# Two gate stages of a graph network kernel: six product slots, third additions on GpSimd, a place of its own for each fold and sum

## The reference, cut to what matters

```
h3 = h.reshape(B, N, F)                         # B = 8, N = 32, F = 768
hg = einsum('bnf,gf->bng', h3, Wg[:, :F])
qg = einsum('blf,gf->blg', q, Wg[:, F:]) + bg   # 64 tokens
attn = sigmoid(hg[:, :, None, :] + qg[:, None, :, :])
qi = einsum('bnlf,blf->bnf', attn, q)
alpha = sigmoid(h3 @ Wq[:, :F].T + qi @ Wq[:, F:].T + bq)
hn = alpha * tanh(qi) + (1.0 - alpha) * h3
```

## Time and profile before

| | us |
|---|---|
| median of three runs | 818.7 |
| lowest and highest | 816.2, 818.98 |
| span of the profiled execution | 814.7 |
| stage 1, first product to last step's sum | 144.15 |
| stage 2, the same | 145.31 |

### The profile page before, as it was taken

One profiled execution on the slowest core, in us unless ns is written; L12 is line 12 of the kernel. 1 busy time (PEld: TensorE's weight loads), 2 busy tenths in 40 slices (PEclk: granted clock), 3 DMA queues, 4 the chain that ended last, 5 costly groups with the idle time before them and its releaser, 6 DMA issues.

```text
span 814.7 us, 10588 instructions
## 1 busy us (share of the span) xinstructions
PE 771.4 (95%) x4195; PEld 640.1 (79%) x4198; DVE 605.2 (74%) x664; ACT 424.9 (52%) x508; POOL 517.8 (64%) x221
## 2 busy tenths in 40 slices
PE   7999999999988999998898889999999999998998
PEld 4669986776645699776666558999999999976897
DVE  8966249999999640889999997764696488666454
ACT  6424446777674342677676725434443444253742
POOL 0625619999998284699999955770685178805500
PEclk9999999999999999999999999999999999999999
DMA  9037526445332464270153328556356546350001
GB/s 365 33 82 234 164 71 176 91 141 156 116 117 78 122 232 150 58 201 1 63 195 117 116 79 281 185 194 230 108 166 207 181 131 218 117 233 0 2 1 39
DMA packets 24409, 111.01 MB, mean 136 GB/s; under 512 B 3620, under 2 KB 6180, under 8 KB 23976
## 3 DMA queue, kind: packets, MB, share of 16 engines
q1 hardware_dynamic: 23240, 104.24, 39.7%
q10 hardware_dynamic: 1120, 6.10, 2.0%
HBM read 100.63 MB, written 0.79 MB: 124 GB/s over the span
## 4 chain that ended last, share of the span: by engine, by line
PE 62%; DVE 19%; POOL 13%; ACT 3%; issue 2%; DMA 0%; DVEq 0%; ACTq 0%
PE ps L1098 28%; DVE prod L1995 11%; POOL prod L593 8%; PE ps L1064 8%; PE ps L1129 5%; DVE qi_t L2013 4%; PE ps L1611 3%; POOL prod L596 2%; PE ps L1389 2%; PE ps L1256 2%; PE ps L1277 2%; PE ps L1679 1%; PE ps L1436 1%; PE ps L1257 1%; PE ps L1326 1%
## 5 line engine op out<-in xcount | busy, mean ns | idle before, releaser
L581 POOL TENSOR_TENSOR w_lo<-w_raw,w_hi 128x1536 fp32r<-128x1536 f32 x49 | 183.7, 3762 | 141.1 <-ACT w_hi L677 141.0
L593 POOL TENSOR_TENSOR prod<-prod 128x1024 f32<-128x1024 f32 x94 | 223.1, 2396 | 26.8 <-DVE prod L1995 26.6
L810 ACT ACTIVATE prod<-ps 128x1024 f32<-128x1024 f32 x192 | 187.4, 1023 | 68.6 <-PE ps L1389 56.0
L1995 DVE TENSOR_TENSOR prod<-prod,ps 128x2048 f32<-128x2048 f32 x96 | 217.7, 2279 | 5.5 <-ACT prod L810 3.5
L677 ACT ACTIVATE w_hi<-w_raw 128x1536 fp32r<-128x1536 f32 x60 | 88.9, 1488 | 119.1 <-PE ps L1098 108.7
L1389 PE MATMUL ps<-sel_pair,h_and_q 128*128 128x512 f32 x384 | 128.2, 446 | 16.7 <-ACT prod L810 16.5
L1098 PE MATMUL ps<-w_hi,yt_hi 128*128 128x384 f32 x480 | 122.9, 336 | 0.1
L1098 PE MATMUL ps<-w_lo,yt_hi 128*128 128x384 f32 x480 | 121.9, 334 | 0.0
L1098 PE MATMUL ps<-w_hi,yt_lo 128*128 128x384 f32 x480 | 121.8, 334 | 0.0
L1389 PEld LDWEIGHTS ps<-sel_pair,h_and_q 128*128 128x128 f32 x384 | 66.5, 189 | 52.5 <-ACT prod L810 32.3
L1064 PE MATMUL ps<-w_raw,h_t 128*128 128x384 f32 x312 | 106.5, 486 | 0.0
(11 more groups left out here) (260 smaller groups left out, 1104.4 us busy)
## 6 DMA issues: line engine op xcount, KB each, us to landing
w_raw<-weights SPq DMA_DIRECT2D x105, 768.0 KB, 4.4
wa_in<-weights SPq DMA_DIRECT2D x6, 768.0 KB, 5.9
w_gat<-weights SPq DMA_DIRECT2D x6, 768.0 KB, 7.9
w_query<-weights SPq DMA_DIRECT2D x3, 768.0 KB, 11.6
h_and_q<-stage_hi SPq DMA_DIRECT2D x24, 96.0 KB, 2.1
h_and_q<-stage_lo SPq DMA_DIRECT2D x24, 96.0 KB, 2.2
a_vec<-gat_vectors ACTq DMA_DIRECT2D x1, 2048.0 KB, 9.6
q_t<-queries ACTq DMA_DIRECT2D x1, 1536.0 KB, 10.5
```

The costliest lines, as they stand in the source:

```text
L581: pool.tensor_tensor(Wl[:, j, :], raw_slab(U, 0, j), Wh[:, j, :], ALU.subtract).then_inc(w_lo_by_pool, 1)
L593: pool.tensor_tensor(v[:, :, 0:32], v[:, :, 0:32], v[:, :, 32:64], ALU.add).then_inc(folded_once, 1)
L810: act.activation(slot_view(s)[:, :, 32 * u:32 * u + 32], args.rearrange("p b (n l) -> p (b n) l", l=LH), ACT.Sigmoid).then_inc(sigmoid_rea ...
L1995: TT(slot_view(s), slot_view(s), ps[:, 6, o:o + L].unsqueeze(1).broadcast_to([P, NB, L]), ALU.mult).then_inc(products_ready, 1)
```

## The change

1. `PSLOTS` goes from 4 to 6. The first five slots lie over the split weights and on into the next region, the sixth over part of the split state. To make room, `h_t` moves by 6144 bytes, the two halves of `yt_hi` and `yt_lo` change places (`v % 2` becomes `1 - v % 2`), and the attention layers at the end use a view of their own, `h_t_attention`, at the old place.
2. A slot is laid out as two contiguous halves of tokens, [2, 32 nodes, 32 tokens], instead of [32 nodes, 64 tokens]. The sigmoid writes a half in one run, the first addition reads two runs of 1024, and the product reads the query row as two halves.
3. A fourth kind, "H": GpSimd adds 8 to 8 after the second addition (256 numbers), and VectorE sums 8 tokens a node. The kinds are written out step by step (T tensor, V vector, G the old "pool").
4. The fold of each tensor step, the second addition and the sum each have a place of their own, in tables. Every second addition in them stands at its own step. The counting of semaphores follows the tables.
5. There is a path for first additions by DMA (`BY_DMA`); both of its lists are empty, so all first additions are on GpSimd.

```diff
-PSLOTS = 4
+PSLOTS = 6
-FOLD_AT = [(5, 8, 11, 14, 15, 17, 20, 22, 23, 26, 35, 44, 46),
-           (5, 8, 9, 11, 12, 14, 15, 17, 18, 20, 21, 23, 26, 35, 38, 41)]
-ALONE = [(4, 10, 16, 25, 27, 28, 30, 34, 37, 40, 42, 45), (25, 27, 28, 30, 34, 40, 42, 44)]
...
-REST_AT = [[s + (3 if KIND[i][s] == "tensor" and KIND[i][s + 1] != "tensor" else 2) for s in range(STEPS - 1)] for i in range(2)]
+KIND = ["VGGVVTHTGVGTGVTVTHVTHVTGGVHTVVTGTGVVHVTHVTTVGTH",
+        "VGVHVTHTTVTHVTGTTVTGVVVTHGHTVTGTVTGTVGTVGVTGGTH"]
+BY_DMA = [(),
+          ()]
+FOLD_AT = [{8: 5, 11: 7, 14: 11, 17: 14, 20: 16, 23: 19, 26: 22, 31: 27, 34: 30, 35: 32, 41: 38, 44: 41, 46: 42, 47: 45},
+           {8: 5, 10: 7, 12: 8, 14: 10, 17: 13, 19: 15, 21: 16, 23: 18, 26: 23, 31: 27, 34: 29, 35: 31, 38: 33, 40: 35, 41:
+           38, 46: 42, 47: 45}]
...
+REST_AT = [[(), (), (0,), (1,), (2,), (), (4,), (3,), (5,), (6,), (8,), (7, 9), (10,), (), (), (11, 12), (), (13,), (14,),
+           (15, 17), (16,), (18,), (), (19, 20, 21), (), (23,), (22,), (24,), (25, 26), (), (), (27, 28), (), (), (29, 30),
+           (31,), (32, 33, 34), (), (35,), (36, 37), (), (38, 39), (40,), (), (41,), (43,), (42,), (44,), (45, 46)],
+           [(), (), (0,), (), (1, 2), (), (3,), (4,), (5, 6), (), (7,), (9,), (8,), (11,), (10,), (12,), (), (13, 14), (),
+           (15,), (), (16, 17), (19,), (18, 20), (), (21, 22), (24,), (23, 25), (), (), (26,), (27, 28), (), (30,), (29, 32),
+           (31,), (), (), (33, 34), (37,), (35, 36), (38, 39), (), (40,), (), (41,), (42, 43), (44,), (45, 46)]]
...
-        PR = sb("prod", [P, PSLOTS, 2048], F32, wh_off)
+        PR = [sb(f"prod{k}", [P, 2, NB, LH], F32, wh_off + 8192 * k if k < 5 else g_off + 16384) for k in range(PSLOTS)]
-        HT = sb("h_t", [P, KC, N], F32, y_off)
+        HT = sb("h_t", [P, KC, N], F32, y_off + 6144)
+        HA = sb("h_t_attention", [P, KC, N], F32, y_off)
...
+            def first_fold(i, s):
...
+                    pool.tensor_tensor(v[:, 0], v[:, 0], v[:, 1], ALU.add).then_inc(folded_once, 1)
+            def second_fold(i, s):
+                v = slot_view(s)[:, 0]
+                wait_folded(pool, i, s)
+                pool.tensor_tensor(v[:, :, 0:16], v[:, :, 0:16], v[:, :, 16:32], ALU.add).then_inc(folded_twice, 1)
+                if KIND[i][s] == "H":
+                    pool.wait_ge(folded_twice, second(i, s))
+                    pool.tensor_tensor(v[:, :, 0:8], v[:, :, 0:8], v[:, :, 8:16], ALU.add).then_inc(folded_thrice, 1)
...
                     if s >= PSLOTS:
                         if u == 1:
-                            act.wait_ge(folded_once, (STEPS - 1) * i + (s - PSLOTS + 1))
-                        elif KIND[i][s - PSLOTS] == "tensor":
-                            act.wait_ge(fold_ready, count_kind(i, s - PSLOTS, "tensor"))
+                            wait_folded(act, i, s - PSLOTS)
+                        elif KIND[i][s - PSLOTS] == "T":
+                            act.wait_ge(fold_ready, by_tensor(i, s - PSLOTS))
                         else:
-                            act.wait_ge(qi_ready, STEPS * i + (s - PSLOTS + 1))
+                            act.wait_ge(qi_ready, reduced(i, [s - PSLOTS]))
...
-                    for past in (s - 3, s - 2):
-                        if past >= 0 and REST_AT[i][past] == s:
-                            reduce(past)
+                    for past in REST_AT[i][s]:
+                        reduce(past)
...
                 reduce(STEPS - 1)
-                reduce(STEPS - 2)
+                for past in REST_AT[i][STEPS]:
+                    reduce(past)
```

More of the change, by code:

```diff
@@ new lines, with numbered @@
+REST_AT = [[(), (), (0,), (1,), (2,), (), (4,), (3,), (5,), (6,), (8,), (7, 9), (10,), (), (), (11, 12), (), (13,), (14,),
[5 rows of a table added]
+def numbered(keys):
+    return {s: n + 1 for n, s in enumerate(keys)}
+FIRST_BY_POOL = [numbered(s for s in range(STEPS - 1) if s not in BY_DMA[i]) for i in range(2)]
+DMA_BEFORE = [sum(s % PSLOTS == k for s in BY_DMA[0]) for k in range(PSLOTS)]
+SECOND = [numbered(s for at in SECOND_AT[i] for s in at) for i in range(2)]
+THIRD = [numbered(s for s in SECOND[i] if KIND[i][s] == "H") for i in range(2)]
@@ L81 @@
+FOLDED = [numbered(FOLD_AT[i].values()) for i in range(2)]
+REDUCED = [numbered([s for at in REST_AT[i][:STEPS] for s in at] + [STEPS - 1] + list(REST_AT[i][STEPS])) for i in range(2)]
 QUERY_EVENTS = [0, 1, 5, 6]
 HEAD_EVENTS = [(2, 3, 4), (7, 8, 9)]
-BANK7 = [sorted([(s, "fold", s - 3) for s in FOLD_AT[0]] + [(29, "q", 0), (32, "q", 1), (38, "h", 0), (40, "h", 1)]),
-         sorted([(s, "fold", s - 3) for s in FOLD_AT[1]] + [(29, "q", 0), (32, "q", 1), (43, "h", 0), (45, "h", 1)])]
+BANK7 = [sorted([(at, "fold", s) for at, s in FOLD_AT[0].items()] + [(29, "q", 0), (32, "q", 1), (38, "h", 0), (40, "h", 1)]),
+         sorted([(at, "fold", s) for at, s in FOLD_AT[1].items()] + [(29, "q", 0), (32, "q", 1), (43, "h", 0), (45, "h", 1)])]
@@ L321, in build @@
         products_ready = sem("products_ready")
+        dma_folded = [sem(f"dma_folded{k}") for k in range(PSLOTS)]
         folded_once = sem("folded_once")
         folded_twice = sem("folded_twice")
+        folded_thrice = sem("folded_thrice")
         fold_ready = sem("fold_ready")
@@ L422, in place_of, with wait_folded, second, third @@
             return t, f, 4 * t + bb, bb
-        def count_kind(i, s, kind):
-            return sum(k == kind for g in range(i) for k in KIND[g]) + sum(k == kind for k in KIND[i][:s + 1])
+        def wait_folded(eng, i, s):
+            if s in BY_DMA[i]:
+                k = s % PSLOTS
+                before = DMA_BEFORE[k] if i == 1 else 0
+                eng.wait_ge(dma_folded[k], 16 * (before + sum(q % PSLOTS == k and q <= s for q in BY_DMA[i])))
+            else:
+                eng.wait_ge(folded_once, (len(FIRST_BY_POOL[0]) if i == 1 else 0) + FIRST_BY_POOL[i][s])
+        def second(i, s):
+            return (len(SECOND[0]) if i == 1 else 0) + SECOND[i][s]
+        def third(i, s):
+            return (len(THIRD[0]) if i == 1 else 0) + THIRD[i][s]
+        def by_tensor(i, s):
+            return (len(FOLDED[0]) if i == 1 else 0) + FOLDED[i][s]
+        def reduced(i, steps):
+            return STEPS * i + max(REDUCED[i][s] for s in steps)
         def head_views(g):
@@ L644, in _ @@
                 for s in range(STEPS - 1):
-                    fold(i, s)
+                    first_fold(i, s)
+                    for q in SECOND_AT[i][s]:
+                        second_fold(i, q)
                     if s == 34:
@@ L1441, in turn_queries @@
                     bank7_free(at_)
-                    pe.wait_ge(qi_ready, STEPS * i + HALF)
+                    pe.wait_ge(qi_ready, reduced(i, range(HALF)))
                     f0, f1 = ((0, 4), (4, KC))[part]
@@ L2362, in elu @@
                     dve.wait_ge(elu_exp_ready, n)
-                    dve.scalar_tensor_tensor(out=HT[:, ks, half], in0=elu_t[:, ks, half], scalar=-1.0,
+                    dve.scalar_tensor_tensor(out=HA[:, ks, half], in0=elu_t[:, ks, half], scalar=-1.0,
                                              in1=chunk_tile(6 - 2 * t, KC)[:, ks, :], op0=ALU.add,
```

91 lines of the change are left out of this document (48 added, 43 removed).

## The result

The changed kernel takes 815.91 us (median of 18 runs, 815.06 to 817.16) against 818.45 us for the kernel before (18 runs, 815.91 to 819.46): ratio 0.9978, 95% interval 0.997 to 0.9986. The 2.5 us are clear of noise, but they are no change by the 0.5% that the prediction set itself; the time is 2.0 us under the 817.9 forecast and inside its own range of 815.5 to 820.5. The profiled span went from 814.7 to 814.2 us; forecast was 813.9.

The account below looks back on a forecast made before the run. In the two gate stages three engines are nearly full, VectorE and GpSimd fullest. Gains of at most 1.3 and 1.5 us, with 1.0 us idle kept in each, become -0.3 and -0.5, together -0.8: span 813.9, time 817.9, range 815.5 to 820.5.

Parts of the forecast that it names:

- The fold in step 47: End of both gate stages on TensorE: a fold of 1.71 us between query part and turns delays the last turn.
- Idle time of VectorE: Both gate stages: of VectorE's 4.0 and 6.4 us of idle time, 1.0 us stays in each.
- Costs of single operations: Gate stages: third addition 0.75 us, 256-element sum 0.41, first additions 2.4 and products 2.28 as before.
- GpSimd's end: GpSimd's last addition in each gate stage: its end moves from 262.9 and 480.1 to 260.9 and 474.7 us.
- The distance from the span to the median: Whole kernel: the median lies 4.0 us above the profiled span, taken as fixed; span 813.9 gives time 817.9.
- (a): Stage ends: the fold in step 47 costs nothing, engine sums reach the end; -3.0 and -3.2 us, time 812.5; chance 0.20.
- (c): Contiguous halves aren't free: 96 products 0.05 us dearer or cheaper, +4.8 or -4.8, time 822.7 or 813.1; chance 0.08.
- (b): GpSimd's third additions come late and VectorE stands still, 0.6 us for each of 13: +5.0, time 823.7; chance 0.14.

Follow-up runs that it names:

- Run 1: Changed kernel with step 45 of kind V instead of T in both stages, so no fold in step 47: 812.87 us, ratio 0.9945 to the kernel before.
- run 4: Changed kernel with all 13 steps of kind H made G, so no third additions: 818.11 us, ratio 1.0001 to the kernel before.
- runs 2 and 3: Changed kernel with the tables of the kernel before: with six slots 817.96 us, ratio 0.9999; with four slots (layout alone) 818.03 us, 1.0008.

## Why the prediction came out as it did

**The fold in step 47: right.** From product 46's end to the last turn the prediction had 9.57 and 10.2 us; the trace has 9.64 and 10.23, against 7.86 and 6.85 before. Run 1 takes the fold out and gets 1.71 and 1.81 us. In stage 1 that is all that was added. In stage 2 another 1.6 us are: TensorE's last query part waits for the sum of step 43, which VectorE made ahead of product 46 before and makes behind it now. TensorE there, in the kernel before and in the changed one:

```profile
472.36 1.53 PE L1064 MATMUL ps<-w_raw,qi_t 128*128 128x384 f32 x4 [1.02 <-DVE qi_t L2013]
```

```profile
471.79 1.53 PE L1118 MATMUL ps<-w_raw,qi_t 128*128 128x384 f32 x4 [1.79 <-DVE qi_t L2072]
```

The first starts 1.96 us before product 46 ends, the second 1.02 us after it. No experiment moved that sum back. Fold and sum are why a change that puts VectorE 1.5 and 4.8 us ahead gives so little.

**Idle time of VectorE: right in kind, twice the size.** I kept 1.0 us in each stage; it is 2.2 and 2.1 (of the latter 0.8 ahead of the statistics of the gate's first node tile). The choice of 1.0 had no row behind it, and the 6.4 us of stage 2 before were short too: the trace has 6.8, with 0.3 us of sums waiting for GpSimd that the earlier trace rows leave out. Of stage 1's, 1.9 us is waiting for ScalarE's sigmoid; of the 1.4 us in the earlier trace rows none went, though the slot waits of ScalarE itself did (5.6 us before, none after). Six slots alone took these slot waits away too, and left VectorE's idle time as it was but for the fall of the clock: it was not the slots that made ScalarE late.

**Costs of single operations: right.** Third addition 0.73 us (0.75), 256-element sum 0.41 (0.41), first additions 2.39 and products 2.28 as before. GpSimd's end is 1.4 and 4.5 us earlier, where 2.0 and 5.4 were forecast.

**What was left out: VectorE instructions with two SBUF operands beside GpSimd.** By the prediction's terms and the 1.0 us kept, product 46 was to end at 139.15 and 138.2; it ended at 139.63 and 137.18. Stage 1 is half a microsecond worse than the sum, stage 2 a microsecond better. The kernel before, on VectorE and then GpSimd:

```profile
220.86 1.92 DVE L2025 TENSOR_TENSOR tanh_q<-tanh_q,alpha 128x768 f32<-128x768 f32 x1
...
455.97 1.00 DVE L1848 SCALAR_TENSOR_TENSOR small<-small 128x1 f32<-128x1 f32 x1
```

```profile
220.70 1.27 POOL L596 TENSOR_TENSOR prod<-prod 128x512 f32<-128x512 f32 x1
221.93 3.09 POOL L593 TENSOR_TENSOR prod<-prod 128x1024 f32<-128x1024 f32 x1
...
454.58 2.37 POOL L593 TENSOR_TENSOR prod<-prod 128x1024 f32<-128x1024 f32 x1
```

and the changed kernel on VectorE:

```profile
219.93 1.33 DVE L2084 TENSOR_TENSOR tanh_q<-tanh_q,alpha 128x768 f32<-128x768 f32 x1
...
433.53 1.68 DVE L2084 TENSOR_TENSOR tanh_q<-tanh_q,alpha 128x768 f32<-128x768 f32 x1
...
453.67 0.55 DVE L1902 SCALAR_TENSOR_TENSOR small<-small 128x1 f32<-128x1 f32 x1
```

The Trainium skill, page SBUF — State Buffer, section SBUF: two separate sides, says that VectorE and GpSimd share a port pair, that whichever starts first holds it for its whole instruction while the other is blocked, and that a VectorE instruction with two SBUF inputs needs it. This case's rows agree: one column took 1.98 us, and 0.16 with GpSimd idle; with one SBUF input it took 0.20.

**The distance from the span to the median: the step that failed.** "I take that distance as fixed" put 4.0 us on the changed kernel; it is 1.7 (815.91 less 814.2). The 4.0 were of two different kinds of run. The execution profiled before was at the full clock with a span of 814.7, and the seven other runs of that kernel with spans of 814.6 to 814.9 take 816.36 to 817.08, 1.8 us more than their span for six of them; the median of 818.7 came from longer runs. The forecast span of 813.9 and 1.8 give 815.7. At 0.999 or more on both sides (in different sessions) it is 816.77 against 815.85 us, 0.9, where 0.8 was forecast. The 18 runs of the kernel before beside the result have no clock on record, but the same gap: seven at 815.91 to 817.16 us, median 816.56, and eleven at 818.11 to 819.46. The other 1.6 us of the medians' 2.5 is then that the changed kernel is seldom in the longer group. That the longer group is the one with falls of the clock is shown by its mean clock alone. Two traces show such a fall and its price at that place, 1.3 us at product 46 with six slots alone and 1.0 us of VectorE's time in run 4, where little of it is left at the end. What brings a fall about stays open: the wait for GpSimd, which the change took away, stands ahead of one of these falls and not of the other, and two traces have the wait and no fall.

**The rivals.** (a) fell with run 1, (c) with runs 2 and 3. (b), late thirds, didn't come: the sums waited 0.1 us for GpSimd in all. Run 4 adds that taking the thirds away costs 2.2 us. That goes against the rule of the Trainium skill, page GPSIMD Engine Reference, section Engine selection, that elementwise additions and sums along the free dimension belong on VectorE.

## What to carry to other kernels

When several engines are nearly full, follow the gain to the instruction that leaves the stage, and look at what was put in front of that one: here a fold of 1.7 us a stage and, in stage 2, a sum put behind one more product ate leads of 1.5 and 4.8 us down to -0.3 and 1.4, and leaving the fold out brought more than the change itself. Buffers and the tables that use them are one edit: the slots alone were worth nothing, and the tables with one slot fewer cost 26 us. Before a distance between a profiled span and a median is carried over, compare the granted clock of the profiled run with that of the others.

## What was not expected of the hardware

- A VectorE instruction with two SBUF tensors waits for the end of GpSimd's running instruction and then holds its next: 1.98 us for one column, 1.25 to 2.01 us for 768 columns that take 0.94 when one operand is in PSUM.
- In the middle of a stage TensorE's granted clock can fall to 1.2 GHz for 3 to 4 us: once behind a 2.35 us wait (a fold of 3.24 us instead of 1.95, product 46 1.3 us later), once with no wait over 0.75 us in the 8 us before (a fold of 3.47 us).
- GpSimd's additions take 0.73, 1.31 and 2.39 us for 256, 512 and 1024 elements; the 1024 take the same flat (2.39) and in runs of 32 (2.40).
